# A fused four-layer cross-attention on one core: the second output half moved ahead of V's second half, and two shared PSUM banks exchanged

## The reference, cut to what matters

```python
q, k, v = x @ Wq, ctx @ Wk, ctx @ Wv            # split into 16 heads of 64
logits = q @ k.T * 64 ** -0.5
logits += -20 * (1 - mask)                      # only in the columns of four given tokens
out = (softmax(logits) @ v) @ Wo + bo + x
```

```python
xn = x * rsqrt(mean(x * x) + 1e-5) * norm_w
out = x + (softmax(xn @ wq @ (ctx @ wk).T / 4) @ (ctx @ wv)) @ wo
```

## Time and profile before

| | |
|---|---|
| median of 3 runs | 3469.21 us (3469.16 to 3471.07) |
| profiled execution | 3470.16 us, span 3468.4 us |
| mean granted clock of TensorE | 0.994 |
| PE busy | 3340.8 us, 96% of the span |
| DVE busy | 2374.6 us, 68% |
| ACT busy | 1916.3 us, 55% |
| POOL busy | 2500.5 us, 72% |
| DMA | 42.20 MB, mean 12 GB/s |

### The profile page before, as it was taken

One profiled execution on the slowest core, in us unless ns is written; L12 is line 12 of the kernel. 1 busy time (PEld: TensorE's weight loads), 2 busy tenths in 40 slices (PEclk: granted clock), 3 DMA queues, 4 the chain that ended last, 5 costly groups with the idle time before them and its releaser, 6 DMA issues.

```text
span 3468.4 us, 71567 instructions
## 1 busy us (share of the span) xinstructions
PE 3340.8 (96%) x27754; PEld 1558.5 (45%) x27754; DVE 2374.6 (68%) x4522; ACT 1916.3 (55%) x2464; POOL 2500.5 (72%) x1206
## 2 busy tenths in 40 slices
PE   6999999999987888889999999999999999999998
PEld 3444444444432322234444444444444444444443
DVE  6667766766666788856676766666666666766665
ACT  5455555555545677764555555555545555555554
POOL 6888888888741000028888888888888888888887
PEclk9999999999998999999999999999999999999999
DMA  4000000000000000000000000000000000000000
GB/s 155 1 11 10 1 10 10 10 1 9 6 10 12 8 12 17 17 1 10 10 3 9 10 10 1 10 10 11 1 10 10 2 10 10 10 1 10 3 1 25
DMA packets 50188, 42.20 MB, mean 12 GB/s; under 512 B 4929, under 2 KB 42177, under 8 KB 49857
## 3 DMA queue, kind: packets, MB, share of 16 engines
q1 hardware_dynamic: 49136, 37.08, 3.5%
q10 hardware_dynamic: 720, 0.53, 0.1%
HBM read 32.36 MB, written 2.10 MB: 10 GB/s over the span
## 4 chain that ended last, share of the span: by engine, by line
PE 90%; ACT 3%; POOL 2%; DVE 2%; issue 2%; DMA 0%; SPq 0%; ACTq 0%; DVEq 0%; POOLq 0%
PE ps_j L886 39%; PE ps_st L1035 13%; PE ps_j L1075 11%; PE ps_sm L969 6%; PE ps_j L1086 4%; PE ps_st L1020 3%; PE ps_j L1062 3%; PE ps_j L1095 3%; ACT pt L1555 2%; PE ps_sm L1049 2%; POOL acc L729 2%; PE ps_j L1115 1%; PE ps_st L969 1%; PE ps_j L978 1%; PE ps_j L1131 1%
## 5 line engine op out<-in xcount | busy, mean ns | idle before, releaser
L729 POOL TENSOR_TENSOR acc<-acc,pt 128x1024 f32<-128x1024 f32 x570 | 1365.0, 2395 | 238.1 <-ACT pt L1555 183.7
L1555 ACT ACTIVATE pt<-ps_st 128x1024 f32<-128x1024 f32 x768 | 742.6, 1019 | 440.3 <-PE ps_st L1035 428.5
L2005 DVE CUSTOM_DVE_ANT_0 ps_sm<-ps_sm,bias_m,nmx 128x512 f32<-128x512 f32 x666 | 480.0, 756 | 218.9 <-PE ps_j L969 184.4
L886 PE MATMUL ps_j<-w_h,ctx_h 128*128 128x128 f16 x3072 | 530.5, 219 | 2.3 <-ACT rinv L1571 1.1
L886 PE MATMUL ps_j<-w_l,ctx_h 128*128 128x128 f16 x3072 | 529.4, 219 | 0.0
L886 PE MATMUL ps_j<-w_h,ctx_l 128*128 128x128 f16 x3072 | 529.4, 219 | 0.0
L1075 PE MATMUL ps_j<-pt,v 128*64 128x512 f32 x1792 | 409.2, 598 | 1.4 <-DVE q_l L1901 1.3
L755 POOL TENSOR_TENSOR o_un<-o_un,rinv 128x512 f32<-128x512 f32 x111 | 142.0, 1279 | 340.6 <-ACT rinv L1567 294.8
L2005 DVE CUSTOM_DVE_ANT_0 ps_sm<-ps_sm,bias_m 128x512 f32<-128x512 f32 x486 | 333.9, 705 | 39.8 <-PE ps_j L969 28.7
L2042 DVE RECIPROCAL rinv<-rinv 128x256 f32<-128x256 f32 x190 | 331.4, 1746 | 14.0 <-ACT rinv L1571 4.4
L734 POOL TENSOR_TENSOR p_l<-pt,p_h 128x1024 f16<-128x1024 f32 x156 | 332.7, 2133 | 0.0
(11 more groups left out here) (198 smaller groups left out, 6173.4 us busy)
## 6 DMA issues: line engine op xcount, KB each, us to landing
w_raw<-wk SPq DMA_DIRECT2D x25, 256.0 KB, 2.8
pt<-ctx_t SPq DMA_DIRECT2D x6, 1024.0 KB, 7.2
w_raw<-wv SPq DMA_DIRECT2D x24, 256.0 KB, 3.7
wo_raw<-wo SPq DMA_DIRECT2D x28, 128.0 KB, 2.0
w_raw<-wq SPq DMA_DIRECT2D x24, 128.0 KB, 2.9
k_h<-k_l SPq DMA_DIRECT2D x72, 32.0 KB, 2.0
x<-x_t SPq DMA_DIRECT2D x4, 512.0 KB, 8.3
acc<-ctx_t SPq DMA_DIRECT2D x2, 1024.0 KB, 8.9
```

The costliest lines, as they stand in the source:

```text
L729: G.tensor_tensor(total, first, pt[:, n % RING, :], ALU.add).then_inc(s_acc, 1)
L886: done = MM(dst, l, r, start=first and i == 0, stop=last and i == n - 1)
L1555: A(pt[:, n % RING, :], src.rearrange("p h q -> p (h q)"), ACT.Exp).then_inc(s_exp, 1)
L2005: last = V.tensor_tensor_reduce(out=src, in0=src, in1=bias_m[:, t, half * HALF:(half + 1) * HALF], scale=-1.0, scalar=nmx[:, 0, t, h:h + 1 ...
```

## The change

In each turned slot, TensorE issues out1 directly after block 3 and V's second half after it; DVE adds out1 before it makes ext_q. In `bank_users` the two banks exchange their numbers from slot −1 on, in the turned slots and in the last one. Inside a slot each user but those of the seam keeps its predecessor; in the seam the order of the users becomes out1 behind pva, v1 behind the opening pass of block 3, nm0 behind out1, the next opening pass behind nm0, and the next pvb behind v1.

```diff
@@ -230,20 +230,20 @@
-            a = int(not splits_x(s))
-            opening(0, 0)
-            if far and not a:
-                then("k0", s + 2, 1)
+            a = int(splits_x(s))
+            opening(0, 1)
+            if far and a:
+                then("k0", s + 2, 0)
...
@@ -251,25 +251,25 @@
             if far:
                 then("q0", s + 2, 1 - a)
-                if a:
-                    then("k0", s + 2, 1)
-                then("k1", s + 2, 0)
+                if not a:
+                    then("k0", s + 2, 0)
+                then("k1", s + 2, 1)
             if nxt:
-                then("v0", s + 1, 1)
-            opening(2, 0)
+                then("v0", s + 1, 0)
+            opening(2, 1)
             if past:
-                then("out0", s - 1, 1)
-            then("pva", s, 0)
-            opening(3, 1)
+                then("out0", s - 1, 0)
+            then("pva", s, 1)
+            opening(3, 0)
+            if past:
+                then("out1", s - 1, 1)
             if nxt:
                 then("v1", s + 1, 0)
                 then("nm0", s + 1, 1)
-            if past:
-                then("out1", s - 1, 1)
             continue
...
@@ -1290,12 +1290,12 @@
                 score_block(3)
+                if past:
+                    project_out(s - 1, 1)
                 if nxt:
                     project_v(s + 1, 1, range(0, 2))
                     rows_of_maxima(s + 1, 0)
                     project_v(s + 1, 1, range(2, 4))
-                if past:
-                    project_out(s - 1, 1)
...
@@ -2195,10 +2195,10 @@
                 peak()
                 peak()
+                if past:
+                    add_out(s - 1, 1)
                 if nxt:
                     extra_rows(s + 1)
-                if past:
-                    add_out(s - 1, 1)
```

More of the change, by code:

```diff
@@ L232, in bank_users @@
         if s == N - 1:
-            then("pvb", s - 1, 0)
-            then("sum", s - 1, 1)
-            then("out0", s - 1, 0)
-            then("out1", s - 1, 1)
+            then("pvb", s - 1, 1)
+            then("sum", s - 1, 0)
+            then("out0", s - 1, 1)
+            then("out1", s - 1, 0)
             continue
@@ L266, in bank_users @@
                 then("nm0", s + 1, 1)
-            if past:
-                then("out1", s - 1, 1)
             continue
         if s == -1:
-            for kind, p, bank in (("bias", 2, 0), ("v0", 0, 1), ("bias", 3, 0), ("bias", 4, 0), ("k0", 1, 1), ("bias", 5, 0),
-                                  ("bias", 6, 0), ("k1", 1, 1), ("bias", 7, 0), ("q0", 1, 0), ("v1", 0, 1), ("nm0", 0, 0)):
+            for kind, p, bank in (("bias", 2, 1), ("v0", 0, 0), ("bias", 3, 1), ("bias", 4, 1), ("k0", 1, 0), ("bias", 5, 1),
+                                  ("bias", 6, 1), ("k1", 1, 0), ("bias", 7, 1), ("q0", 1, 1), ("v1", 0, 0), ("nm0", 0, 1)):
                 then(kind, p, bank)
```

## The result

| | before | after |
|---|---|---|
| median (range), runs | 3469.18 us (3466.73 to 3471.07), 4 | 3486.78 us (3485.25 to 3487.43), 4 |
| profiled execution | 3470.16 us, span 3468.4 | 3487.43 us, span 3485.6 |
| mean granted clock | 0.994 | 0.995 |

The ratio is 1.0051, 95% interval 1.0033 to 1.0068: the change makes the kernel 17.6 us slower. I had said 3489.7 us.

The account below looks back on a forecast made before the run. PE, busy 96% of the span, bounds the kernel. Seam stalls of 20.6 + 1.0 + 0.3, less 1.0 for POOL and 0.4 at slot 48, give +20.5 us: median 3489.7 us, 8-in-10 range 3477 to 3501.

Parts of the forecast that it names:

- Swapping the roles of the banks: Between block 0 and block 3, allotments keep their predecessors under other numbers: 0 us; slot 48's opening pass gains 0.4 us.
- out1 ahead of V: At the seam, three out1 matmuls move 1.65 us forward on PE; the new waits for ACT and maxima are hidden: 0 us.
- nm0 waits for the add: At the seam, nm0 needs DVE's add of out1, which stands behind block 3's maxima: PE stalls 0.24 us per turned slot.
- the twin: The same DVE-to-PE pattern elsewhere in the earlier trace: a waiting L978 matmul starts 0.15 us after DVE's operation ends.
- the three late ones: Slots 12, 56 and 79, where the last maximum is late: a stall of 0.32 us each, 1.0 us together.
- The bounds, 0.15 and 0.38: Seam stall per slot: 0.15 us with the shortest DVE-to-PE way, 0.38 if the add starts only after the accumulator read.
- The wait for POOL absorbs 1.0 us: Slots 78 to 81: PE's wait for o_l before out0, 3.7 us, shrinks by the preceding seam's stall, four times 0.24.
- ext_q is no second wait: Next slot's first matmul: ext_q, now behind the add on DVE, is in time by 0.34 us, costing 0 us.
- R1: Not slower: DVE's 1.24 us seam idle goes and block 2's waits shrink by 8 us, 3461 or 3482 us; 5%.
- R2: A second wait: the add starts 0.14 later or ext_q is late, 0.38 us per slot or more, 3502 to 3508; 7%.
- R3: A short pause in each slot lowers PE's granted clock; 2% of the turned slots is 55 us, 3545 us; 2%.
- What would show it: Signs: idle of 0.24 us before L978 put down to DVE's L2050, slot of 29.95 us, new wait row of some 20 us.

Follow-up runs that it names:

- e1_rename: The changed kernel's exchanged bank numbers, but the old order of out1, V and nm0 on PE and DVE: 3467.56 us, ratio 0.9998 to before.
- e3_between: The changed kernel, but DVE adds out1 between the two halves of block 3's closing maxima instead of behind both: 3468.08 us, ratio 0.9996 to before.
- the dose: Three kernels: the changed kernel with nm0 after 12, 26 or 28 of V's 48 matmuls instead of 24: 3546.48, 3475.38 and 3467.01 us.
- n12_sooner: The changed kernel with nm0 12 matmuls sooner, after 12 of V's 48 instead of 24: 3546.48 us, ratio 1.0228 to before.
- n26_half: The changed kernel with nm0 2 matmuls later, after 26 of V's 48 instead of 24: 3475.38 us, ratio 1.0023 to before.
- n28: The changed kernel with nm0 4 matmuls later, after 28 of V's 48 instead of 24: 3467.01 us, ratio 0.9996 to before.
- e7: e3_between with v_l also moved between the two halves of block 2's opening maxima on DVE: 3458.95 us, ratio 0.9975 to before.
- e8: The kernel before, with only v_l moved between the two halves of block 2's opening maxima on DVE: 3459.51 us, ratio 0.9976 to before.
- e2: The kernel before with its old bank numbers, but the change's new order in the seam on PE and DVE: 3486.93 us, ratio 1.0051 to before.

## Why the prediction held, step by step

- *What bounds the kernel.* Right: PE at a clock of 1.00 in the slots, and 0.2 us per slot is 17.6 us of the end.
- *Swapping the roles of the banks, 0 us.* Right (e1_rename, interval 0.9989 to 1.0007); its −0.4 at slot 48 measured −0.43.
- *out1 ahead of V, 0 us by itself.* Right (e3_between). The copy of pva on ACT was done at 708.42, 1.45 before out1's first matmul; V's first matmul came without a pause at 710.53; V's late copy left ACT 0.71 us of idle.
- *nm0 waits for the add: 0.24 us per seam.* The mechanism is right (e3 and the dose), the size was 0.03 too large. The latency from the add's end to nm0 was the 0.15 of the twin. What was off is when nm0 is due: I reckoned 1.98 us after out1's first matmul, and it is 711.87 − 709.87 = 2.00, since out1's first matmul holds PE for 0.23 (709.87 to 710.10), not 0.215; and the last read came 2.49 us before the next slot (713.73 − 711.24), which less the stall is 2.28, as in the earlier trace rows. Over the 89 seams of the two stretches block 3 is 18.6 us longer (0.21 each), where I had 20.6 + 1.0 with the three late ones. Those (slots 12, 56, 79) measured 0.26 to 0.28, not 0.32. Slot 28, which I had at 0.3, pauses 0.29; it lies in the middle stretch.
- *The bounds, 0.15 and 0.38.* 0.38 was the case in which the add waits for the end of the accumulator read. The row at 711.24 says again that it isn't so here: the read and the add start together, 0.08 us before the recorded end of the custom operation ahead of them (710.59 + 0.73), and the seam stalls 0.21. I had quoted the Trainium skill (VectorE: DVE Perf Modes, "The DRAIN you can't avoid") as against this, and left out that the same paragraph goes on to say that a next operation that is not held starts earlier. So the trace does not contradict the page.
- *The wait for POOL absorbs 1.0 us.* Wrong in size: it absorbed 0.4. The earlier trace rows is a row of PEld, 3.7 us in four places; the row of PE itself for the same wait was 1.9 us in two places. In slots 78 and 79 only the weight load idled, beneath a matmul that still ran, so there was no pause of PE to shrink (block 2 took 6.70 before and after). In slots 80 and 81 it fell from 7.13 to 6.81 and from 7.95 to 7.84. The row of PE for these slots, in before and in after:

```profile
PE ps_j L886 <- POOL o_l L760: 1.9, 2, 1.4
...
PE ps_j L886 <- POOL o_l L760: 1.5, 2, 1.3
```

- *ext_q is no second wait.* Right: ext_q ended at 713.25, 0.48 before the L1020 matmul that reads it.
- *The sum.* 18.6 for the 89 seams, −0.4 for POOL and −0.4 for slot 48 make 17.8, and the two stretches of slots show 5.60 + 11.99 = 17.6; with slot 28's 0.3 that is 17.9 where I had 20.5. The difference is mostly the 0.03 in 90 seams (2.7), and 0.6 the other way from POOL. That the medians are 17.6 apart, so near to the slots' 17.9, is in part luck: the runs of one kernel lie up to 5 us apart (before, 3466.8 to 3471.6).
- *The rivals.* R1: DVE's 1.24 us of idle only moved, from out1 to the next slot's first opening pass, so nothing behind it came sooner; block 2 still took 6.18 us, and before v_l DVE waits for ACT as it did (161.8 us in 78 places in both). R2: no pause at L1020. R3: the clock stayed at 1.00 with a pause of 0.21 us in every slot, and even with 0.88, as the window of n12_sooner's slots 0 to 27 shows (the row below). The Trainium skill (TensorE: Matmul & The Clock Gate, "A second HAM failure mode: psum-queue depth-cycling") tells of such pauses bringing the clock down; in the turned slots no run here did that.

```profile
48.73:908.57 859.84, 833.56 (x7129) 409.28 (x7128) 568.44 (x1191) 446.27 (x589) 714.24 (x339) 1.00 0.03 8
```

- *What would show it.* One sign was named wrongly: the new row is one of PEld that names "issue", not DVE's L2050, since most of a pause of 0.21 us (0.16) lies under the record of the matmul before it, and PE gets no row.

## What to carry to other kernels

When a buffer passes to a new user, ask what its last reader stands behind in its own engine's queue, not how long that reader takes: the add took 0.69 us, but it could not begin before maxima that end late in the slot. Before the change nm0 got its bank from block 3's opening pass, which had been read by then, and the bank that out1 left went to a user behind block 0 of the next slot. An idle of an engine off the path (DVE's 121.9 us for out1) is no gain to be had: here it only moved to another wait of DVE, at a price of 17.6 us on PE, and the 9 us that could be had lay in moving one DVE operation by one place.

## What the runs showed of the hardware beyond that

- From the end of a DVE operation that reads PSUM to the start of the matmul that waited for it: 0.15 us in after, 0.14 in n12_sooner and n26_half, 0.15 in the earlier trace rows.
- A pause of PE of 0.21 us gives no row of PE in the list of waits, only one of PEld that says "issue"; one of 0.88 us at the same instruction gives a row of PE with its true cause. The difference is what the record of the matmul before it hides, 0.16 us. And a row of PEld counts idle of the weight load that PE never felt (3.7 us in slots 78 to 81, of which PE's own row has 1.9). The distance of two matmuls' starts is the safe measure.
- The start up to slot 0 (48.7 to 51.6 us) and slots 28 to 47 (663.9 to 669.2 us) differ by some 3 and 5 us from one profiled execution to the next, while the turned slots repeat within 0.1 us over 28 of them. So changes of a few us are read from the slots, not from the total. Both follow the granted clock. By the clock's records in the traces, TensorE spent 30.7 us of slots 28 to 47 at the lower of its two levels (1.2 GHz) in before and in n12_sooner, where they took 668.3 and 669.2 us (n12's with a pause of 0.9 in slot 28); 23.9 in e3, n28, e7 and e8 (665.5 to 665.8); 20.5 in after and e2 (665.2 and 665.3); 17.0 in n26 (664.2); and 13.6 in e1 (663.9). Ahead of slot 0 it was there for nothing in before, n12 and n28 (48.7 to 49.2 us), for 3.4 us in e2, e3, e7 and e8 (50.3 to 50.8) and for 6.8 us in after, e1 and n26 (51.4 to 51.6). With one profiled execution of each kernel this is a match of numbers and no experiment; why the clock fell where it did was not tried.
